# Attention and ternary FFN on one core: weighted sums in pairs, and a new order on every engine

## The reference

```python
x = x + attention(layernorm(x), ctx)          # 32 batches, x and ctx 128 x 512 each
    q, k, v = proj(Wq, bq, x), proj(Wk, bk, c), proj(Wv, bv, c)     # 8 heads of 16, over 512 positions
    q, k = rope(q, 8), rope(k, 8)
    p = softmax(q @ k.T / 4)                  # 512 x 512 for each head
    out = proj(Wo, bo, p @ v)
x = x + ffn(layernorm(x))
    gate, up = bitlinear(x, w_gate), bitlinear(x, w_up)             # 512 -> 2048
    y = silu(gate) * up
    out = bitlinear(fwht(y), w_down)          # Hadamard transform over 2048, then 2048 -> 512
bitlinear(x, w) = act_quant(x) @ weight_quant(w).T
act_quant(x)    = clip(round(x * s), -128, 127) / s,  s = 128 / max(max|x| of the row, 1e-5)
weight_quant(w) = clip(round(w / m), -1, 1) * m,      m = mean|w|
```

## Time and profile before

| | |
|---|---|
| median of 3 runs | 1533.31 us (1532.55 to 1535.38) |
| the profiled execution | 1531.52 us, its span 1529.7 us |
| busy in the span | PE 93%, DVE 86%, ACT 71%, POOL 72%, weight loads 49% |
| one step in the middle (615.08 to 658.63) | 43.55 us |
| granted TensorE clock | half of full speed from 55 to 90 us, full or nearly so from 95 us on, lower again at the end |

### The profile page before, as it was taken

The page is one execution under the profiler, slowest core; times in us unless marked ns, Lnnn a source line. Parts: engine busy times, 40 slices in busy tenths (PEclk is TensorE's granted clock), DMA queues, the critical chain, the costliest instruction groups (busy, mean ns, idle before and its releaser), DMA issues.

```text
span 1529.7 us, 30990 instructions
## 1 busy us (share of the span) xinstructions
PE 1424.7 (93%) x11042; PEld 743.8 (49%) x11042; DVE 1322.4 (86%) x2331; ACT 1082.5 (71%) x1777; POOL 1098.7 (72%) x812
## 2 busy tenths in 40 slices
PE   1688999999999999999999999999999999999983
PEld 1215455545555555455555544555555444555442
DVE  2768899999999999999999999999999999998641
ACT  3586677778777777787777777877777777777762
POOL 4124777887777778877777788777777887777674
PEclk9688999999999999999999999999999999999996
DMA  8861434434234344343244443332434443323000
GB/s 211 223 124 37 66 63 77 70 63 69 61 60 77 63 77 76 58 70 63 58 76 63 77 77 61 66 65 61 70 64 77 77 68 59 69 46 47 15 8 14
DMA packets 81112, 108.12 MB, mean 71 GB/s; under 512 B 9664, under 2 KB 59200, under 8 KB 79936
## 3 DMA queue, kind: packets, MB, share of 16 engines
q1 hardware_dynamic: 77744, 93.56, 35.4%
q10 hardware_dynamic: 3216, 12.58, 2.3%
HBM read 38.73 MB, written 8.39 MB: 31 GB/s over the span
## 4 chain that ended last, share of the span: by engine, by line
PE 71%; ACT 12%; DVE 5%; issue 4%; POOL 4%; DMA 2%; SPq 0%; POOLq 0%; ACTq 0%; DVEq 0%
PE s L469 12%; PE ring L525 12%; PE pv L484 12%; PE s L439 11%; PE ring L560 7%; PE ring L536 6%; ACT region L712 4%; PE ring L413 3%; PE ring L493 2%; ACT parts L779 2%; PE ring L547 2%; PE ring L427 2%; ACT y_last L753 1%; ACT y_last L771 1%; DVE maxima L1009 1%
## 5 line engine op out<-in xcount | busy, mean ns | idle before, releaser
L1009 DVE TENSOR_REDUCE maxima<-s 128x1 bf16<-128x512 f32 x1024 | 668.3, 682 | 60.1 <-PE s L439 55.6
L712 ACT ACTIVATE region<-s 128x512 f32<-128x512 f32 x1024 | 576.0, 597 | 133.3 <-PE s L469 123.8
L439 PE MATMUL s<-region 96*128 96x512 bf16 x1024 | 374.3, 391 | 21.7 <-DVE maxima L1009 11.5
L1274 POOL TENSOR_TENSOR region<-region,th 128x512 f32<-128x512 f32 x128 | 161.8, 1273 | 297.1 <-DVE th L1104 295.3
L469 PE MATMUL s<-region 97*128 97x512 bf16 x1024 | 362.2, 384 | 10.0 <-ACT region L712 4.8
L1265 POOL TENSOR_TENSOR region<-region 128x512 f32<-128x512 f32 x192 | 260.3, 1356 | 12.8
L484 PE MATMUL pv<-region,v_ext 128*17 128x512 f32 x2048 | 264.1, 599 | 0.0
L1266 POOL TENSOR_TENSOR region<-region 128x512 f32<-128x512 f32 x192 | 243.9, 1270 | 0.0
L439 PEld LDWEIGHTS s<-region 96*128 96x128 bf16 x1024 | 99.8, 98 | 198.6 <-DVE maxima L1009 74.2
L469 PEld LDWEIGHTS s<-region 97*128 97x128 bf16 x1024 | 93.2, 98 | 187.7 <-ACT region L712 154.1
L1263 POOL TENSOR_TENSOR region<-region 128x1024 f32<-128x1024 f32 x64 | 149.4, 2355 | 0.1
(11 more groups left out here) (104 smaller groups left out, 1812.0 us busy)
## 6 DMA issues: line engine op xcount, KB each, us to landing
region<-parts SPq DMA_DIRECT2D x384, 128.0 KB, 4.8
x_in<-in_x SPq DMA_DIRECT2D x32, 256.0 KB, 2.6
c_in<-in_ctx SPq DMA_DIRECT2D x32, 256.0 KB, 2.9
rope_c<-region SPq DMA_DIRECT2D x64, 128.0 KB, 2.4
x_res<-in_x SPq DMA_DIRECT2D x32, 256.0 KB, 2.6
out<-o_sb SPq DMA_DIRECT2D x32, 256.0 KB, 2.4
region<-in_wg_t ACTq DMA_DIRECT2D x1, 2048.0 KB, 9.2
region<-in_wu_t ACTq DMA_DIRECT2D x1, 2048.0 KB, 7.3
```

The lines of the kernel that those rows point to most:

```text
L439: pe.matmul(s1[p][:, :], q_stack[k][0:STACK, h, 128 * c:128 * (c + 1)], k_stack[k][0:STACK, h, :], start=True, stop=True).then_inc(s1_full ...
L712: act.activation(probs[:, n % 8, :], s2[n % 2][:, :], ACT.Exp, scale=SCALE).then_inc(exp_done, 1)
L1009: dve.reduce_max(maxima[:, c, h:h + 1], s1[p][:, :], AXX).then_inc(s1_max[p], 1)
L1274: pool.tensor_tensor(zj, zj, th[:, j % 2, :], ALU.mult).then_inc(glu_done, 1)
```

## The change

Three edits, and with them new lists in all `step` functions (other positions for most calls, up3 in the same step as the rest of gate and up, other positions in `RING`, so other banks):

1. `weigh(b, v)` makes the sums of two chunks of keys, u = 2v and 2v + 1, one after the other; there are four calls a step, and each waits for eight exponentials.
2. `whole_y` is gone. `clip_y` reads the rounded f32 y, takes the minimum with 1.5 * 2**23 + 127, subtracts 1.5 * 2**23 and writes bf16. `y_out` waits for `yq_done` in place of `whole`.
3. The ones of k's first two buffers are set on all partitions by `ones_rows(t + 6, k)`, called in GpSimd's step (FIRST is now -6, so in its first one); SP waits for them before the first stacking DMA of each of the three buffers, TensorE no longer does.

```diff
-FIRST, LAST = -3, B + 5
+FIRST, LAST = -6, B + 5
...
-                    if b == 2:
-                        sp.wait_ge(third_ones_set, 1)
+                    if b < 3:
+                        sp.wait_ge(ones_rows_set, b + 1)
...
-            def weigh(b, u):
+            def weigh(b, v):
...
-                g, c = u // KC, u % KC
...
-                if c == 0:
-                    wait(pe, pv_turned, 2 * b + g)
-                pe.wait_ge(exp_done, 32 * b + 4 * (u + 1))
-                for i in range(4):
-                    last = pe.matmul(pv[32 * i:32 * i + DH + 1, :], v_ext[b % 2][:, c, 4 * g + i, :],
-                                     probs[:, (4 * u + i) % 8, :], start=(c == 0), stop=(c == KC - 1))
-                last.then_inc(pv_done, 1)
+                for u in (2 * v, 2 * v + 1):
+                    g, c = u // KC, u % KC
+                    if c == 0:
+                        wait(pe, pv_turned, 2 * b + g)
+                    pe.wait_ge(exp_done, 32 * b + 8 * (v + 1))
+                    for i in range(4):
+                        last = pe.matmul(pv[32 * i:32 * i + DH + 1, :], v_ext[b % 2][:, c, 4 * g + i, :],
+                                         probs[:, (4 * u + i) % 8, :], start=(c == 0), stop=(c == KC - 1))
+                    last.then_inc(pv_done, 1)
...
-            def whole_y(b, j):
-                if not live(b):
-                    return
-                full(act, f"yT{j}", b - 1)
...
-                act.wait_ge(rounded, 2 * b + j + 1)
-                act.activation(yq[:, 1024 * j:1024 * (j + 1)], ys[:, 1024 * j:1024 * (j + 1)], ACT.Copy, bias=-ROUND) \
-                   .then_inc(whole, 1)
...
-                dve.wait_ge(whole, 2 * b + j + 1)
-                half = yq[:, 1024 * j:1024 * (j + 1)]
-                dve.tensor_scalar(half, half, 127.0, None, ALU.min).then_inc(yq_done, 1)
+                full(dve, f"yT{j}", b - 1)
+                if b == 0:
+                    dve.wait_ge(ternary, UPTO[3])
+                dve.wait_ge(rounded, 2 * b + j + 1)
+                dve.tensor_scalar(yq[:, 1024 * j:1024 * (j + 1)], ys[:, 1024 * j:1024 * (j + 1)],
+                                  ROUND + 127, ROUND, ALU.min, ALU.subtract).then_inc(yq_done, 1)
...
+            def ones_rows(b, k):
+
+                if b == 0:
+                    unstaged(pool, k)
+                    pool.memset(k_stack[k][:, :, :], 1.0).then_inc(ones_rows_set, 1)
...
+                ones_rows(t + 6, 0)
+                ones_rows(t + 6, 1)
                 rstd1(t + 1)
+                ones_rows(t - 1, 2)
```

More of the change, by code:

```diff
@@ L640, in step @@
+                gate_up(t - 2, "gate", 2)
+                project(t + 1, "q")
+                score_max(t, 5)
+                scores(t - 1, 8)
+                score_max(t, 6)
+                scores(t - 1, 9)
+                weigh(t - 1, 0)
+                scores(t - 1, 10)
                 score_max(t, 7)
-                scores(t - 1, 8)
+                y_transpose(t - 3, 0)
                 score_max(t, 8)
                 project(t + 1, "k")
-                scores(t - 1, 9)
-                scores(t - 1, 10)
+                scores(t - 1, 11)
@@ L666, in _ @@
+                weigh(t - 1, 1)
             for t in range(FIRST, LAST):
@@ L758, in y_out @@
                     return
-                wait(act, whole, 2 * (b - 1) + j // 2 + 1)
+                wait(act, yq_done, 2 * (b - 1) + j // 2 + 1)
                 if b == 0:
@@ L865, in step @@
-                exps(t - 1, 2)
-                load_weights(t + 3, 0, 1)
+                sign_piece(t - 2, 2, 3)
                 exps(t - 1, 3)
                 exps(t - 1, 4)
-                sign_piece(t - 1, 1, 2)
+                sign_piece(t, 0, 2)
+                round_y(t - 3, 0)
                 tanh(t - 2, 0)
                 exps(t - 1, 5)
-                sign_piece(t - 2, 2, 3)
                 tanh(t - 2, 1)
+                exps(t - 1, 6)
                 sign_piece(t - 2, 2, 4)
-                round_y(t - 3, 0)
+                load_weights(t + 3, 0, 1)
@@ L876, in step @@
+                exps(t - 1, 7)
+                round_y(t - 3, 1)
                 sign_piece(t - 2, 2, 5)
-                exps(t - 1, 6)
-                whole_y(t - 3, 0)
-                sign_piece(t - 2, 2, 6)
-                abs_piece(t - 1, 2, 2)
-                exps(t - 1, 7)
+                sign_piece(t - 1, 1, 2)
                 exps(t - 1, 8)
-                tanh(t - 2, 2)
+                exps(t - 1, 9)
+                load_weights(t, 1, 1)
+                exps(t - 1, 10)
                 sign_piece(t - 1, 1, 3)
-                abs_piece(t + 2, 0, 0)
@@ L886, in step @@
-                exps(t - 1, 9)
-                exps(t - 1, 10)
                 exps(t - 1, 11)
-                round_y(t - 3, 1)
-                abs_piece(t - 1, 2, 3)
+                yT_out(t - 3, 0)
                 exps(t - 1, 12)
                 exps(t - 1, 13)
-                sign_piece(t, 0, 2)
+                tanh(t - 2, 2)
                 exps(t - 1, 14)
-                yT_out(t - 3, 0)
-                abs_piece(t - 1, 2, 4)
+                sign_piece(t - 2, 2, 6)
+                exps(t - 1, 15)
@@ L897, in step @@
+                abs_piece(t + 1, 0, 1)
                 tanh(t - 2, 3)
-                exps(t - 1, 15)
-                whole_y(t - 3, 1)
+                abs_piece(t - 1, 2, 2)
                 exps(t - 1, 16)
+                exps(t - 1, 17)
                 first_part(t + 1)
-                exps(t - 1, 17)
                 exps(t - 1, 18)
-                sign_piece(t - 2, 2, 7)
-                sign_piece(t, 0, 3)
+                abs_piece(t, 1, 0)
+                abs_piece(t + 1, 0, 2)
@@ L1139, in step @@
             def step(t):
+                rope_sin(t + 1, 1)
+                reduce_scores(t, 9)
+                reduce_scores(t, 10)
+                reduce_scores(t, 11)
+                rope_cos(t + 1, 1)
+                reduce_scores(t, 12)
+                reduce_scores(t, 13)
+                glu(t - 2, 2)
                 half_gates(t - 2, 3)
-                glu(t - 2, 2)
+                round_piece(t, 0, 3)
                 reduce_scores(t, 14)
```

252 lines of the change are left out of this document (111 added, 141 removed).

## The result

| | before | after |
|---|---|---|
| time, median of 4 runs each, us | 1534.35 | 1568.81 (1565.68 to 1573.37) |
| ratio, 95% interval | | 1.0226 (1.0196 to 1.0256) |
| span of the profiled execution, us | 1529.7 | 1566.1 |
| a regular step in the middle, us | 43.55 | 44.46 |
| 28 steps, `mix` 1 of batch 1 to `mix` 1 of batch 29, us | 1222.4 | 1255.5 |

The profiled execution is 36.4 us longer: 4.8 in the start, 33.1 in the 28 steps, -1.5 at the end.

What follows compares the result with a forecast made beforehand. A closed loop over VectorE, ScalarE and GpSimd was taken to set the step: -0.2 + 1.05 + 0.35 - 0.54 = +0.66 us, times 29 is 19.1, with +1.5 and -0.8 +19.8, so 1553 us; range 1516 to 1570.

Steps and rivals of the forecast that it cites:

- (c): Rival: both clips hold GpSimd, or ScalarE's waits for pairs join the loop; +1.2 us a step, 1569 us; 10%.
- (d): Rival: TensorE's rate decides, pairs give 0.7 us a step, the end 0.8; 1512 us, 1523 if half arrives; 22%.
- the loop as I had it: Likeliest case: the loop over VectorE, ScalarE and GpSimd grows 0.66 us a step; 1545 to 1561 us; 38%.
- a closed loop: Chain from one second mix to the next over VectorE, ScalarE and GpSimd, 43.54 us, claimed to set the step.
- Part 1: Weighted sums in pairs: 0.7 us a step less on TensorE, ScalarE idle 0.2 to 0.7 three times; counted 0.
- Part 2: VectorE and ScalarE's path from mix 1 to glu 0: ends 0.2 us earlier, at best 0.65, at worst 0.
- Part 3: VectorE between the two glu: norm1_apply and one more reduction add 1.05 us to GpSimd's stretch, between 0.9 and 1.2.
- the first clip: f32 clip directly behind glu 1, taking 0.70 us: holds GpSimd's second product 0.35 us, between 0 and 0.55.
- the old hold: GpSimd's subtraction beside the first clip before, 1.81 us against 1.27: the 0.54 us it lost goes away.
- The second clip: Clip among GpSimd's additions: taken as 0 for GpSimd since it lost before, up to 0.55 us if it wins.
- Start and end: Start +1.5 us from other positions, between -3 and +6; end about 0.8 us less, the last down products freed earlier.
- rival (b): The same loop, but the f32 clip does not hold GpSimd: +0.31 us a step, 1543 us; 18%.

Runs made afterwards that it cites:

- c1: Kernel before with four of the 16 down matmuls left out, 0.87 us a step less on TensorE; 1531.5 us, ratio 0.9991.
- c2: Kernel before with GpSimd's turn done for q alone, some 1.1 us a step less on GpSimd; 1527.8 us, ratio 0.9961.
- b3: Kernel before with norm1_apply moved from ahead of the first half_gates to behind the second glu; 1555.3 us, ratio 1.0141.
- b2: Kernel before with the weighted sums alone changed to pairs, four times a step; 1668.8 us, ratio 1.0872.
- a5: a2 with the pairs undone, eight single weighted sums a step; 1629.2 us, ratio 1.0624.
- v2: a2 with VectorE's work regrouped: only norm1_apply between the first two glu, reductions moved back, also behind glu 3; 1583.9 us, ratio 1.0327.
- a3: Changed kernel with the clip as before: ScalarE's whole_y back, VectorE clips bf16 in the same two places; 1555.1 us, ratio 1.0136.
- a1: Changed kernel with norm1_apply and one reduction moved from between the first two glu to behind the second; 1581.6 us, ratio 1.0317.
- a12: Changed kernel with the edits of both a1 and a2; 1568.8 us, ratio 1.0224.
- a2: Changed kernel with the k projection and second rope_sin moved earlier, so the shift DMAs are issued 1.9 us earlier; 1559.9 us, ratio 1.0170.
- b1: Kernel before with the clip alone changed: whole_y gone, VectorE clips from f32 in the two old places; 1545.5 us, ratio 1.0070.
- a23: Changed kernel with the edits of both a2 and a3 (shift early, bf16 clip); 1551.6 us, ratio 1.0115.

## Why the prediction was right in direction, and 16 us short

The forecast was 1553 us, and 1568.8 lies 1.2 us inside its outer range, 1516 to 1570. That range had been drawn wide for rivals (c) and (d); the range of the loop as I had it, 1545 to 1561, does not hold the time. The direction and the loop came out for the reason given; that the outer range held is in part luck, since the shift was not in the sum.

**The loop.** Right for a change that makes it longer. TensorE's rate was rival (d); c1 takes 0.87 us a step from TensorE and nothing comes. But the reading "a closed loop" left out that a second path, over the last pair and VectorE, was 0.17 us behind it (c2). For a longer loop that matters less, and this change made it longer. Had I forecast a gain from a shorter loop, I would have been wrong, as in b3.

**Part 1.** Counted 0 for TensorE, and nothing in the runs speaks against it, but none of them has a price of the pairs by itself (b2, a5). The waits on the pairs are there, 77 us of ScalarE in 68 places, but up to 1.81 us each, where I had 0.2 to 0.7. They didn't reach the loop in this order; in v2 they did.

**Part 2.** Forecast 0.2 us earlier, 14.9 to 15.1 us from `mix` 1 to the end of `glu` 0: it is 634.24 - 619.19 = 15.05, 0.08 earlier. `turn_back` stands behind a second reduction and comes 0.97 behind `mix` 1 instead of 0.72; from there to the end of `glu` 0 it is 0.33 shorter.

**Part 3 and the first clip.** Forecast 1.05 + 0.35 for the products, and -0.54 for the old hold. Measured: 3.92 - 2.67 = 1.25, and 1.81 to 1.27, -0.54. Of the 1.25, 0.92 is the later start of the second product (forecast 1.05, between 0.9 and 1.2). The f32 clip takes 0.69 (forecast 0.70), and the product beside it 1.59 instead of 1.27, a hold of 0.32 (forecast 0.35); with the bf16 clip in the same place it is 1.33 (a3). What a1 and a12 add: the 1.05 is no price that an undo gives back. Behind it, `glu` 3 was ready only 0.4 us before the fourth product needed it (a2), and VectorE's work moved there took that.

**The second clip is the term that failed in the step.** I took 0, "since it lost here". It lost again, 3.04 us on VectorE, but when it gets in, GpSimd's next instruction is held: 1.59 instead of 1.34. The prediction's "and GpSimd nothing" was a misreading: the subtraction at 638.11 before had taken 1.34 where others take 1.27. b1 shows the same 0.25 in the old order. 28 x 0.25 = 7 us. The other misses in the step cancel: +0.12 in part 2, -0.15 in part 3 and the first clip, +0.03 spread. Rival (c) had both clips holding GpSimd, at 1.2 us a step and 1569; its mechanism is half of what happened, at 0.9 a step, and that its time was met is due to the shift.

The SBUF page of the Trainium skill (SBUF — State Buffer, Who interferes with whom) has the shared ports kept by whoever issued first. The trace agrees for the second clip: it starts beside a running GpSimd instruction, lasts until a gap between two of them (in after, from 652.93 until the one at 655.49), and what starts there pays. It does not agree for the first clip of before, which started 0.26 us behind GpSimd's subtraction by the records and still took 0.40, while the subtraction took 1.81; there the measurement decides.

**The shift is the term that was missing.** I had not looked at which VectorE instruction SyncE's shift waits for. It is the second `rope_sin`. That went from 622.70 to 641.31 in the steps shown, 20.3 us behind `mix` 1 before and 22.1 after, and `turn` with its DMAs lost 1.24 us of slack. a2 gives what moving it back returns, 10.3 us, of which 6.8 are the waits themselves.

**Start and end.** Forecast +1.5 and -0.8, measured +4.8 and -1.5. In the start of after (GpSimd and TensorE) stand

```profile
65.02 2.13 POOL L1301 TENSOR_TENSOR parts<-rope_c,parts 128x1024 bf16<-128x1024 f32 x1 [4.43 <-ACT parts L768]
...
83.42 1.03 PE L439 MATMUL s<-region 96*128 96x512 bf16 x2 [7.38 <-DMA region<-parts]
```

`third_part` waited 4.43 us for its cast, which stood behind three sums over weight pieces: the cast started at 63.90 us instead of 60.35, and in all kernels of the new order at 63.9 to 66.2, of the old one at 58.2 to 61.1. The second batch's first scores came at 83.42 instead of 79.70. How much of the 4.8 us at `mix` 1 this is stays open, since the start also varies with the execution. c1 and c2, in the old order, reached the same `mix` 1 at 168.9 and 167.6, where before has 164.3; their granted clock from 30 to 60 us was 0.61, before 0.88. At a like clock there (0.88 to 0.89) before, b1 and b3 took 164.3 to 164.7, a2 169.2 and a23 170.7, which speaks for the order. In two kernels of the new order the clock does not show: after had 1.00 there and a3 0.56, and they took 169.1 and 168.1. (Before, the clock was also down to 0.50 from 120 to 130 us, which the table ahead of the prediction leaves out.)

The forecast was 19.1 for 29 steps, +1.5 and -0.8. In the trace it is 28 x 0.91 = 25.5 for the regular steps, 7.6 for the long ones, +4.8 and -1.5: 36.4. Of the 33.1 in the steps, the late shift and the f32 clip hold 23.2 together (a23; 10.3 and 14.6 each alone, a2 and a3), and 9.9 are left, 0.35 us a step: the longer stretch between the two `glu` less what part 2 and the old hold give back. That is the mechanism of rival (b), forecast at 0.31. No version here beats the kernel before.

## What to carry to other kernels

When a loop over several engines is read from a trace, take work off each engine in turn (c1, c2): it tells which path binds and how far the next one is behind, and here that was 0.17 us. The mean busy shares and the chain that ended last did not tell it. In an order packed like this, a wait that appears is not a price that can be taken back; undoing it moves it. For each instruction that moves, look for the DMA that waits on it, and compare the time from issue to use with the longest landing in the steps, not the median.

## What was not expected of the hardware

- Two transfers of 128 KB, issued 0.6 us apart, have landed 2.9 to 3.0 us after the first issue in most steps and up to 4.76 in after. With 3.85 us from that issue to the use they were late in 8 of 28 steps; with 5.09 (before) and 5.70 (a2) never, and with 4.35 in neither a12 nor v2.
- A clip that loses against GpSimd grows from 0.40 to 1.95 us in bf16 before, and to 3.17 in a3; from 0.69 to 3.45 in f32 in after. So the place counts for more than the type. GpSimd's next instruction takes 1.34 (bf16) and 1.60 (f32) there against 1.27, and 1.73 in a12. A clip that starts 0.26 us behind a GpSimd instruction and gets in at once costs GpSimd 0.54 in bf16 and 0.79 in f32 (1.81 and 2.06 against 1.27, before and b1); one that starts 0.23 ahead of it costs 0.06 and 0.32 (1.33 and 1.59, a3 and after).
- A `norm1_apply` beside a product of GpSimd goes with 1.44 us for the product instead of 1.27 (after and b3). In after the wait behind it hid that.
- By the shares of the chain that ended last TensorE had 71% before (the line below). Taking 0.87 us a step from TensorE changed nothing all the same (c1).

```profile
PE 71%; ACT 12%; DVE 5%; issue 4%; POOL 4%; DMA 2%; SPq 0%; POOLq 0%; ACTq 0%; DVEq 0%
```
